# The last Fourier stage joined to the token phase, and PE slots moved in the Mamba phase

## What is computed

```python
# layer 0: two Mamba blocks, then fusion
for i in range(2): seq = seq + mamba_block(seq, ...)   # norm, in_w, conv of 4, silu, x/dt projections,
                                                       # scan of 16 states per channel, * silu(z), out_w
# layer 1: x + two SS2D blocks of the group-normalised x
# layer 2: Fourier attention and a quantised feed-forward
h = relu(bn1(ln(t) @ w1)); X = fft(h, axis=1)          # 4096 points = 64 x 64
x = relu(Re(X) * rd - Im(X) * id + rb) + 1j * relu(...)
t = t + bn2(real(ifft(x)) @ w2)
t = t + ffn(ln(t))                                     # 96 -> 384 -> 96, 8-bit operands, 16-bit sums
# layer 3: linear attention (no softmax) and a second feed-forward
t = t + attn(ln(t)); t = t + ffn(ln(t))
```

## Time and profile before

| | |
|---|---|
| median of 3 runs | 7334.84 us (7332.33 to 7348.52) |
| the profiled execution | 7338.5 us, its span 7336.6 us |
| Mamba phase | about 0 to 2832 us of the span |
| last Fourier stage | 6744.1 to about 6858 us |
| token phase | 6858.7 to 7336.6 us |
| busy share of the span | DVE 87%, PE 82%, ACT and POOL 74% |

### The profile page before, as it was taken

The page is one execution under the profiler, slowest core; times in us unless marked ns, Lnnn a source line. Parts: engine busy times, 40 slices in busy tenths (PEclk is TensorE's granted clock), DMA queues, the critical chain, the costliest instruction groups (busy, mean ns, idle before and its releaser), DMA issues. The chain is left out here.

```text
span 7336.6 us, 105959 instructions
## 1 busy us (share of the span) xinstructions
PE 6001.3 (82%) x18352; PEld 2099.6 (29%) x18352; DVE 6352.8 (87%) x7494; ACT 5456.3 (74%) x11126; POOL 5456.9 (74%) x4289
## 2 busy tenths in 40 slices
PE   7888888888888884588888888888888777889787
PEld 2222222222222221222222222222222112478443
DVE  6999999999999997299999999999999994633657
ACT  7888888888888884377888888888888874322567
POOL 5888898888888884188999999998999992000526
PEclk8999999899999997788999999999999887998789
DMA  4544454454445444488888888888888883245401
GB/s 97 116 103 105 115 116 103 106 118 113 103 105 116 115 103 113 112 186 190 190 192 192 192 194 191 191 193 194 195 195 195 193 189 94 88 156 158 130 1 35
DMA packets 583999, 1025.47 MB, mean 140 GB/s; under 512 B 105769, under 2 KB 140766, under 8 KB 580670
## 3 DMA queue, kind: packets, MB, share of 16 engines
q1 hardware_dynamic: 583710, 1022.58, 58.9%
HBM read 845.35 MB, written 176.96 MB: 139 GB/s over the span
## 5 line engine op out<-in xcount | busy, mean ns | idle before, releaser
L1648 POOL TENSOR_TENSOR scan_prod<-scan_hs,scan_BC_rep 128x512 f32<-128x512 f32 x1536 | 1931.9, 1271 | 200.1 <-DVE scan_hs L1572 196.8
L664 POOL TENSOR_TENSOR mamba_prod<-mamba_hs,mamba_BC_rep 128x512 f32<-128x512 f32 x1536 | 1916.8, 1271 | 210.5 <-DVE mamba_hs L621 207.8
L621 DVE TENSOR_TENSOR_SCAN mamba_hs<-mamba_dA,mamba_carry,mamba_dbx 128x512 f32<-128x512 f32 x1152 | 1423.9, 1263 | 1.6
L1417 ACT ACTIVATE scan_dA<-scan_delta_rep,scan_a_neg 128x512 f32<-128x512 f32 x1536 | 1094.6, 714 | 303.8 <-DVE scan_hs L1572 296.0
L1193 PE MATMUL scan_u_rep<-scan_du,scan_sel 96*128 96x512 f32 x1536 | 898.7, 671 | 402.4 <-DVE scan_hs L1572 401.7
L546 ACT ACTIVATE mamba_dA<-mamba_delta_rep,mamba_a_neg 128x512 f32<-128x512 f32 x1536 | 1092.6, 712 | 116.1 <-DVE mamba_hs L621 112.8
L1572 DVE TENSOR_TENSOR_SCAN scan_hs<-scan_dA,scan_carry,scan_dbx_even 128x512 f32<-128x512 f32 x768 | 973.7, 1268 | 47.1 <-ACT scan_carry L1397 40.5
L1572 DVE TENSOR_TENSOR_SCAN scan_hs<-scan_dA,scan_carry,scan_u_rep 128x512 f32<-128x512 f32 x768 | 973.6, 1268 | 0.2
L600 DVE TENSOR_TENSOR mamba_dbx<-mamba_u_rep,mamba_BC_rep 128x512 f32<-128x512 f32 x1152 | 774.8, 673 | 83.4 <-PE mamba_u_rep L332 70.4
L332 PE MATMUL mamba_u_rep<-mamba_du,mamba_sel 96*128 96x512 f32 x768 | 461.9, 685 | 315.4 <-DVE mamba_hs L621 314.7
L1528 DVE TENSOR_TENSOR scan_dbx_even<-scan_u_rep,scan_BC_rep 128x512 f32<-128x512 f32 x768 | 517.9, 674 | 129.0 <-DMA scan_BC_rep<-proj_rows 123.4
(11 more groups left out here) (304 smaller groups left out, 10594.4 us busy)
## 6 DMA issues: line engine op xcount, KB each, us to landing
scan_BC_rep<-proj_rows SPq DMA_DIRECT2D x1024, 256.0 KB, 6.5
scan_delta_rep<-proj_rows SPq DMA_DIRECT2D x1024, 192.0 KB, 3.5
mamba_BC_rep<-bc_units SPq DMA_DIRECT2D x512, 256.0 KB, 8.0
mamba_delta_rep<-delta_units SPq DMA_DIRECT2D x512, 192.0 KB, 3.6
proj_rows<-scan_dbc SPq DMA_DIRECT2D x256, 224.0 KB, 7.1
delta_units<-mamba_delta SPq DMA_DIRECT2D x128, 192.0 KB, 5.3
by_n<-fin_res SPq DMA_DIRECT2D x32, 768.0 KB, 3.2
fmid_src<-by_n SPq DMA_DIRECT2D x32, 768.0 KB, 5.2
```

The costliest lines, as they stand in the source:

```text
L621: nc.vector.tensor_tensor_scan(hs[:, s % RING_H], dA[:, s % RING_A], dbx_bank(s)[:], carry[:, bass.ds(at, 1)], op0=ALU.mult, op1=ALU.add). ...
L664: pool.tensor_tensor(prod[:, (G * u + s) % RING_P], hs[:, s % RING_H], BC_rep[:, u, QUADS + s % QUADS], ALU.mult).then_inc(s_prod, 1)
L1417: nc.scalar.activation(dA[:, (2 * k + s) % 4], delta_rep[:, k, s // 2], ACT.Exp, scale=a_neg[lay][:, at:at + 1]).then_inc(s_dA, 1)
L1648: pool.tensor_tensor(prod[:, (G * k + s) % RING_P], hs[:, (G * k + s) % RING_H], BC_rep[:, k, 2 + s % 2], ALU.mult).then_inc(s_prod, 1)
```

## The change

Part 1. `fourier_out_phase` is removed; a class `FourierOut` does the same chunks inside the token phase, all 32 before the first step of the first feed-forward. The tokens stay in the SBUF tile `x`: the stores to and loads from the second DRAM tensor are gone. Its constants and rings share the space of `xn` (tile `room`), so the memset of the ones in `xn` moves from step 8 to the last step of the first feed-forward. `quantise` moves from step 2 to before step 0. The image of the tokens is now loaded right after the first spectrum chunk of the image, for the first image too (before: after the fourth chunk). The feed-forward's weights are loaded after the eighth chunk.

Part 2. In the Mamba phase, slots change: on PE the z product of the second half from 0 to 1, both projections to slot 4 (from 3 and 5), the mean from 8 to 10, the variance from 10 to 12, the output product from 9 to 7; on ACT `to_raw` to 4, 6, 7 (from 3, 4, 6), the square from 13 to 15, rsqrt from 16 to 17, `to_raw` 0 from 23 to 22, `evict_y` from 10 to 8 and from 20 to 19, `evict_out` from 15 to 19; on POOL the gates from 6 to 5 and from 18 to 20, `normalise` from 12 to 14.

```diff
             def next_step(s, lay, m, v):
-                if s == 0:
+                if s == 1:
                     project_z(lay, m, 1)
-                elif s == 3:
-                    project(lay, m, v, 0)
-                elif s == 5:
-                    project(lay, m, v, 1)
+                elif s == 4:
+                    for half in range(2):
+                        project(lay, m, v, half)
...
-                if s == 8:
+                if s == 10:
                     mean(m, v)
-                elif s == 10:
+                elif s == 12:
                     var(m, v)
...
-                    if s == 9 and prev is not None:
+                    if s == 7 and prev is not None:
                         project_out(prev, n - 1, 1 - u, 0)
                         project_out(prev, n - 1, 1 - u, 1)
...
-                if s in (3, 4, 6):
-                    to_raw(lay, m, {3: 1, 4: 2, 6: 3}[s])
+                if s in (4, 6, 7):
+                    to_raw(lay, m, {4: 1, 6: 2, 7: 3}[s])
...
-                if s == 13:
+                if s == 15:
                     square(m)
-                elif s == 16:
+                elif s == 17:
                     rsqrt(m)
...
-                elif s == 23:
+                elif s == 22:
                     to_raw(lay, m, 0)
...
-                    if s == 10 and prev is not None:
+                    if s == 8 and prev is not None:
                         evict_y(n - 1, 1)
-                    if s == 20:
+                    if s == 19:
                         evict_y(n, 0)
-                    if s == 15 and prev is not None:
+                    if s == 19 and prev is not None:
                         evict_out(n - 1)
...
-                    if s == 6 and prev is not None:
+                    if s == 5 and prev is not None:
                         gate(n - 1, 1 - u, 1)
-                    if s == 18:
+                    if s == 20:
                         gate(n, u, 0)
...
-                if s == 12:
+                if s == 14:
                     normalise(m)
...
+class FourierOut:
+    def load(self, sp, c):
+        b, q = divmod(c, self.NC8)
+        wait(sp, self.s_y_ps, c - self.RING + 1)
+        part = self.spectrum[b].rearrange("(n r) k h -> n (r k) h", r=2)
+        sp.dma_start(self.src[:, c % self.RING], part[q * self.NC8:(q + 1) * self.NC8].rearrange("n p h -> p n h")
+                     ).then_inc(self.s_in[c % self.RING], 16)
+        if q == 0:
+            sp.dma_start(self.k.x[:, b * L:b * L + L], self.x_in(b)).then_inc(self.s_x[b], 16)
...
+        def transformed(pe, n):
+            if n == 0:
+                pe.wait_ge(tiles.s_set, 2)
+            if n % CH == 0:
+                pe.wait_ge(fourier.s_res, fourier.NC8 * (n // CH + 1))
+            if n == 0:
+                pe.wait_ge(fourier.s_o, fourier.CHUNKS)
...
+            fourier.load_weights(sp)
+            for c in range(fourier.NC8):
+                fourier.load(sp, c)
             first.load_weights(sp)
+            for c in range(fourier.NC8, fourier.CHUNKS):
+                fourier.load(sp, c)
...
                 first.gpsimd(pool, t)
-                if t == 8:
+                if t == first.STEPS - 1:
+                    pool.wait_ge(fourier.s_res, fourier.CHUNKS)
                     pool.memset(xn[C:E], 1.0).then_inc(s_ones, 1)
...
+            fourier.vector_begin(dve)
+            for c in range(AHEAD):
+                fourier.vector(dve, c)
+            first.quantise(dve)
             for t in range(first.STEPS):
-                if t == 2:
-                    first.quantise(dve)
```

More of the change, by code:

```diff
@@ L1826, with __init__ @@
     STEPS = UNITS + 14
-    def __init__(self, p, tag, tiles, w, ready):
-        self.nc, self.k, self.w, self.ready = p.nc, tiles, w, ready
+    def __init__(self, p, tag, tiles, hid, out, w, ready):
+        self.nc, self.k, self.hid, self.out, self.w, self.ready = p.nc, tiles, hid, out, w, ready
+        self.HB, self.OB = len(hid), len(out)
         sb = lambda n, *a: p.sb(f"{tag}_{n}", *a)
@@ L1889, in tensor @@
             pe.wait_ge(self.s_h8, n + 1)
-            wait(pe, self.s_o16, n - 1)
+            wait(pe, self.s_o16, n - self.OB + 1)
             for j in range(J):
-                last = nc.tensor.matmul(k.out[n % 2][0:C], self.w2q[:, j], k.h8[:, n % 2, j],
+                last = nc.tensor.matmul(self.out[n % self.OB][0:C], self.w2q[:, j], k.h8[:, n % 2, j],
                                         start=(j == 0), stop=(j == J - 1))
@@ L1906, in scalar @@
             wait(act, self.s_y16, n - 1)
-            nc.scalar.activation(k.out16[:, n % 2], k.out[n % 2][0:C], ACT.Copy).then_inc(self.s_o16, 1)
+            nc.scalar.activation(k.out16[:, n % 2], self.out[n % self.OB][0:C], ACT.Copy).then_inc(self.s_o16, 1)
         n = t - 5
@@ L2055, in token_phase @@
         x = tiles.x
-        xn = p.sb("xn", [E, B * L])
+        room = p.sb("room", [128, B * L])
+        xn = room[0:E]
         w_kv = p.sb("w_kv", [E, 2 * C])
@@ L2075, in token_phase @@
         s_o, s_res, s_store = p.sem("o"), p.sem("res"), p.sem("store")
-        def loaded(pe, n):
+        def transformed(pe, n):
             if n == 0:
                 pe.wait_ge(tiles.s_set, 2)
-                pe.wait_ge(s_x[0], 16)
-            elif n == 2:
-                pe.wait_ge(s_x[1], 16)
-            elif n % CH == 0:
-                pe.wait_ge(s_x[n // CH + 1], 16)
+            if n % CH == 0:
+                pe.wait_ge(fourier.s_res, fourier.NC8 * (n // CH + 1))
+            if n == 0:
+                pe.wait_ge(fourier.s_o, fourier.CHUNKS)
         def attended(pe, n):
             pe.wait_ge(s_res, n + 1)
-        first = FeedForward(p, "first", tiles, w_first, loaded)
-        last = FeedForward(p, "last", tiles, w_last, attended)
+        fourier = FourierOut(p, tiles, room, tiles.hid, x_in, spectrum, w_fourier)
+        AHEAD = fourier.CHUNKS
+        first = FeedForward(p, "first", tiles, tiles.hid, tiles.out, w_first, transformed)
+        last = FeedForward(p, "last", tiles, tiles.hid, tiles.out, w_last, attended)
         norm = AttentionNorm(p, tiles, xn, first)
@@ L2203, in _ @@
             act.wait_ge(tiles.s_set, 2)
+            fourier.scalar_begin(act)
+            for c in range(AHEAD):
+                fourier.scalar(act, c)
             for t in range(first.STEPS):
+                if AHEAD + t < fourier.CHUNKS:
+                    fourier.scalar(act, AHEAD + t)
                 first.scalar(act, t)
@@ L2249, in _ @@
             nc.vector.memset(tiles.eps[:], 1e-5).then_inc(tiles.s_set, 1)
+            fourier.vector_begin(dve)
+            for c in range(AHEAD):
+                fourier.vector(dve, c)
+            first.quantise(dve)
             for t in range(first.STEPS):
-                if t == 2:
-                    first.quantise(dve)
+                if AHEAD + t < fourier.CHUNKS:
+                    fourier.vector(dve, AHEAD + t)
                 first.vector(dve, t)
@@ L2763, in conv_attn_hybrid @@
     delta_units = scratch("delta_units", 2, 2, C, T)
-    tokens = [scratch(f"tokens{i}", C, B, L) for i in range(2)]
+    tokens = scratch("tokens", C, B, L)
     by_n2 = scratch("by_n2", B, 2 * HW, HW, HID2)
```

172 lines of the change are left out of this document (70 added, 102 removed).

## The result

| | before | changed |
|---|---|---|
| median of 9 executions each, us | 7338.66 (7320.53 to 7350.44) | 7297.78 (7287.03 to 7308.48) |
| ratio, 95% interval | | 0.9945 (0.9936 to 0.9953) |
| profiled execution's own time / span, us | 7338.5 / 7336.6 | 7292.83 / 7291.1 |

The kernel is 40.9 us faster by these medians. That the total came out is not yet a reason to believe the steps; they are read one by one.

A forecast was written before the change was run, and what follows sets the result against it. Bounds: DVE in Mamba, PE fed by DMA in the last Fourier stage, ACT in the first feed-forward. -20 - 14.6 - 13 + 4.5 = -43 us, from 7334.84 to a median of 7292; range 7280 to 7312, leaving out the slow ends.

The forecast's parts named there:

- Step (a): Mamba phase, PE's slots: the block of slot 11 starts up to 1.8 us earlier, ending DVE's waits; -20 us.
- at most 20.9 us: Mamba phase: upper bound on the gain, DVE's waits for PE's replicated block, whatever else the slots do.
- Step (b): Mamba phase, ACT's and POOL's slots: normalise ends 2.5 us later but the scan is not held; cost 0.
- the cover of slot 20: Mamba phase: ACT's decay of slot 20 would still be done 0.7 us before DVE scans with it.
- slower rival: Mamba phase: slot 19 on ACT becomes the bound, delaying slot 20's decay; 7375 us, slower by 0.5%; chance 0.03.
- Step (c): Handover from last Fourier stage to first feed-forward: third xm at about 6857.2 instead of 6871.78; -14.6 us.
- Step (d): First feed-forward: with the memset out of step 8, ACT's idle piece of 12.98 us goes; -13 us.
- Step (e): Last step of the first feed-forward: the memset is not hidden and the first turn waits for it; +4.5 us.
- The rival in which xn is held: End of first feed-forward: the memset also holds DVE's xn, costing 11.8 us; time 7299; chance 0.04.
- Step (f): Last Fourier stage's loop: PE's chunk waits change place, three stores leave; from -8.5 to +4, taken as 0.
- Step (g): Rest of part 1, attention and second feed-forward: only shifted in time, with no term in the sum.

The follow-up runs named there:

- e7: Kernel before with only the output product moved (slot 9 to 7), its eviction of y and gate following; Mamba loop 2818.0 us, before 2760.2.
- e10: Changed kernel with the output product back at slot 9, eviction of y at 10, gate at 6; Mamba loop 2736.5 us, changed 2739.7.
- e8: Kernel before with only mean, variance, square, root and normalise moved to later slots; Mamba loop 2737.4 us, before 2760.2.
- best2: best with e8's Mamba slots and the pieces of x for image 1 moved behind chunk 3; 7292.94 us, ratio 0.9928 to the kernel before.
- best: Changed kernel with e4's edit, x loaded in pieces, and the square ahead of silu(z) in ACT's prologue; 7284.89 us, ratio 0.9936 to the kernel before.
- e3: Changed kernel with the memset of the ones back in step 8 of the first feed-forward; third xm to turn 171.1 us, changed 160.3.
- e4: Changed kernel with the memset in two pieces, the first while the Fourier products run; third xm to turn 156.6 us, changed 160.3.

## Why the prediction was right, step by step

Step (a), PE's slots, -20: right in size, wrong in half of its reason. The loop lost 21.1 us (mean of the six executions with the changed slots 2739.2, of the two with the old ones 2760.3). The prediction said that the wait of 0.95 us for the mean's bank goes "since the output product stands in slot 7 and fills it". It does fill it (2.4 us of waits in e7), but only by making the mean late: alone, that move cost 58 us, and undone in the changed kernel it cost nothing (e10). The moves of the mean and the variance gave the whole gain (e8). The prediction's "at most 20.9 us" was no bound either: the loops of e8, e10 and `best2` are 22.9 to 24.4 us shorter than the old one, some 4 us of which are in no wait of DVE.

Step (a) also left out the prologue, which repeats the slots with no scan to cover them. The first scan came at 67.7, 69.2 and 66.9 us with the old order and at 70.7 to 73.2 with the changed one (seven executions, mean 71.9), 4.0 later. This is the term that the sum lacked. PE's projection and variance there, in before and in the changed kernel:

```profile
35.41 5.75 PE L317 MATMUL mamba_pre<-mamba_xz,mamba_w_proj 96*96 96x512 f32 x8 [2.04 <-ACT mamba_xz L460]
...
46.33 2.02 PE L291 MATMUL mamba_pre<-mamba_sq,mamba_mean_w 96*96 96x512 f32 x2 [1.17 <-ACT mamba_sq L495]
```

```profile
37.09 5.34 PE L317 MATMUL mamba_pre<-mamba_xz,mamba_w_proj 96*96 96x512 f32 x8 [3.26 <-ACT mamba_raw L453]
...
50.65 2.02 PE L291 MATMUL mamba_pre<-mamba_sq,mamba_mean_w 96*96 96x512 f32 x2 [3.90 <-ACT mamba_sq L494]
```

There are two delays. ACT's copy of z (`to_raw`, slot 4 to 6) now stands behind the silu of x, and PE waits for it ahead of the projections, 3.26 us in place of 2.04. With that and what the clock adds, the mean starts at 44.6 to 45.4 us where the projections moved (eight executions) and at 42.6 to 43.2 where they did not (five), 2.0 later. And the square (slot 13 to 15) now stands behind the silu of z (slot 14), two table loads and 3.6 us: from the mean to the convolution are 11.5 us in all nine kernels with that order, 9.6 to 10.4 in the four with the square first, `best` among them. The rest of the 4.0 is the clock under the convolution and the first blocks.

Step (b), 0: right, but its cover was mis-sized. Against scan 16 the normalise ends 1.2 us later than before, not 2.5, and the cover of slot 20 is 3.3 us in the median (4.7 before), not 0.7. The slower rival was further off than it was priced: it took a normalise 4.0 us later to lose 1.5 us a unit.

Step (c), -14.6: measured 22.30 - 7.74 = 14.56. The residual ends at 6821.62 and the third xm starts 6.49 us later; predicted "about 6.5". PE ran at the lower clock (1.99 us a pair). From the last residual's start to the third xm are 7.7 us in all nine executions with the changed token phase and 22.2 to 23.1 in the four with the old one, so 14.9 by the means.

Step (d), -13: right. The 12.98 us are gone, and e3 brings back 12.99.

Step (e), +4.5: 3.7 by e4, of which the prediction had 3.6 as the memset's and the rest as the restart. The rival in which xn is held did not happen: 0.68 us beside the memset. The Trainium skill's rule in "SBUF — State Buffer", "Who interferes with whom", that a two-input tensor_tensor meets only a GpSimd instruction that reads SBUF, agrees with this row; that a cast is held agrees with its 6.89 us.

Steps (d) and (e) together were -8.5; from the third xm to the turn the table shows 169.5 in the mean of four executions and 160.5 in the mean of five, -8.9.

Step (f), 0: the loop took 95.1 us as before in this pair, with 11.1 and 11.9 us of waits in other places; by the means of the same four and five executions it is 1.0 shorter. Not counted was its head, from the first DMA to the first product: 9.4 to 9.9 us in the four, 10.2 to 10.8 in the five, 0.9 more by the means. The tokens' 1.5 MB are now issued between chunks 0 and 1; where they are not, it is 10.1 (`best`) and 9.8 (`best2`), so they are at most a part of it.

Step (g), 0: not shown. Behind the turn are 297.3 us in the mean of the four and 299.9 in the mean of the five, 2.6 more, which may be the clock alone.

So the token part is -14.9 (c) - 8.9 (d, e) - 1.0 + 0.9 (f) + 2.6 (g) = -21.3, predicted -14.6 - 13 + 4.5 = -23.1. With the Mamba part the sum is -21.1 (a, loop) + 4.0 (a, prologue) - 21.3 = -38.4 us, where the two measurements of the whole gave -40.9 and -35.2 and the prediction said -43. The profiled pair would have given -32.0 for the same places and hidden the rest in the clock. Of the 5.8 us by which the measured median stands above 7292, 3.8 are the kernel before, whose median of nine is 7338.66 and not 7334.84. The large terms, (a)'s loop, (c) and (d), were read from waits that went; the prologue's +4.0 and (g)'s +2.6 are in no step, and that they were small is luck.

## What to carry to other kernels

A product that waits in an in-order engine costs all that stands behind it; before filling its wait, look what it waits for and move the product itself to where that is done. Moving a second product into the gap of a first that has not moved can delay the first by more than the gap. And when the order of slots changes inside a loop, read the same order in the prologue, where nothing covers it.

When untouched phases differ between two profiles by as much as touched ones, run the halves alone, side by side, and compare a touched stretch over all executions at hand, not over one pair. And measure a cover (how long a result lies ready before it is read) over many units, not by adding up what stands ahead of it.

## What the runs showed of the hardware

The same instructions in the final convolutions took 252.4 us at a granted clock of 1.00 and 262.4 at 0.96, in executions that entered the phase at the same microsecond. Over the thirteen executions the times are 252.4 or 252.5 (seven), 257.3 to 258.7 (four) and 262.4 (two), and no edit sorts them.

A cast on DVE that starts beside a memset on POOL ends just behind it, at both sizes seen: 384 columns took 6.89 us in place of 0.35 and ended 0.2 us behind the memset, 1536 columns 10.44 in place of 0.94 to 1.5 and ended 0.8 us behind it. In the last Fourier stage PE, busy for 20.45 of 21 us, was granted half its clock (the column before the last two):

```profile
6732.00:6753.00 21.00, 20.45 (x128) 20.45 (x128) 9.45 (x8) 5.41 (x7) 0.00 (x0) 0.50 0.91 210
```
